# Second attention begun in the first experts' last rounds, and biases of several samples as one block-diagonal product

## The chip, the core and the metric

One core of one Trainium2 chip runs the whole program. The metric is the device time in microseconds, the median of several executions. An execution of the profiler is one more run; its trace is what this document reads. TensorE (PE in the rows, PEld its weight loads) multiplies matrices, VectorE (DVE), ScalarE (ACT) and GpSimd (POOL) work elementwise, SyncE (SP) issues most DMAs. Each engine has its own instruction queue and runs it strictly in the order in which the program wrote it; they meet at semaphores.

## The reference

The input x is 64 samples of 8192 numbers. All is float32.

```python
h = tokenizer(x)                      # conv, batch norm, ReLU, max pool, twice; self-attention; conv, norm
h = h + attention_and_mlp(layernorm(h))   # local and linear attention of 8 heads, then an MLP 64-256-64
h = h + experts(layernorm(h))             # 16 experts 64-128-64, two chosen per token, then a layer norm
h = h + attention(layernorm(h))           # 8 heads of width 64 over 512-token rows, softmax, Wout, bout
h = h + small_experts(layernorm(h))       # 32 experts 64-16-64, one chosen per token

# the part of experts() that the change touches:
topk_vals, topk_idx = top_k(x @ gate_w + gate_b, 2)
topk_w = softmax(topk_vals)
expert_out = relu(x @ w1 + b1) @ w2 + b2
y = x + sum(topk_w * expert_out[topk_idx])
out = (y - mean(y)) / sqrt(var(y) + eps) * gamma + beta
```

After the tokenizer, the data are 64 samples of 128 tokens with 64 features each. The kernel treats each sample of 128 tokens for itself: a sample is one tile of 128 partitions by 64.

## The kernel before

The kernel is written instruction by instruction, with an own program for each engine. It is a row of stages, in the list `PHASES`: tokenizer, a norm, first attention (`attention0`), a norm, MLP (`mlp0`), a norm, first experts (`experts0`), a norm (`n5`), second attention (`attention1`), a norm, last experts (`experts1`). Every stage gives each engine a function, and an engine's program is those functions one after another. So the order of the work on an engine is the order in which the code was written, and an engine passes from one stage to the next by itself; only the waits on semaphores hold it. A norm between two stages gathers the per-sample statistics of all 64 samples (VectorE: six small operations and a reciprocal; ScalarE: the square root), so the next stage's input waits for the last group of the stage before.

The tokenizer works in 8 groups of 8 samples (`NG`, `GS`), the others in 16 groups of 4 samples (`TG`, `TS`). Each stage has a `rest(g, b, ...)` per engine, called once for each group, with a hardware loop around the middle groups; steps of neighbouring groups are interleaved there by hand.

- *Tokenizer.* SP loads inputs in halves of a group, two groups ahead; a first block of constants, the rest of the tokenizer's (`load_rest`), and then the constants of all other stages and the experts' weights (`load_layers`). `conv1`, `conv2` and `conv3` are the convolutions on TensorE, `reduce1` and `reduce2` the max pools on VectorE. `fold_w2` prepares the second convolution's weights on VectorE, and stands there ahead of all `reduce1` (L404).
- *First experts.* For each group the input is centred and scaled on GpSimd (`Paired.pool`), transposed on TensorE (`Paired.pe`), copied out by ScalarE (`Paired.act`). `hidden` (L1431) and `out` (L1443) are the products of two experts for four samples; `relu` (L1644) stands between them on ScalarE; `weighted` (L1585) multiplies by the gate weights on VectorE; `add` (L1368, L1371) sums on GpSimd; `fold` (L1397) ends it. `turn_weights` (L1451) transposes the gate weights of each of the four samples, `turned` (L1653) copies them, `biases` (L1459) multiplies each sample's with the experts' output biases `eb2`, in halves of 64 tokens. `sums`, `count_y`, `variance`, `normal`, `result` and `count` on VectorE, `centre` and `scale` on GpSimd and `deviation` on ScalarE are the layer norm, one to two groups later. A `tail` does what is left after the last group.
- *Second attention.* TensorE first multiplies the weights, `wkT` with `wqT` and `wvT` with `wout` (L1893), into two matrices `w_a` and `w_m`, copied out by ScalarE (L1959). GpSimd makes a group's input, `turned` (L1699, L1704, L1812), for two groups ahead of the loop. TensorE transposes it (L1714) and makes four projections (`piece`, L1850 and L1852), each in the same two banks of PSUM, so each waits until ScalarE has copied the one before (L1936, L1941). Then for each sample: scores (`now`, L1862), maximum and difference on VectorE (L1908, L1911), exp on ScalarE (L1948), transposes (`lag1`, L1870), copy (L1953), products with the values (`lag2`, L1884), division (L1916, L1919), and the sums over heads on GpSimd.
- *Last experts.* `biases` (L2049) adds the chosen expert's output bias to each sample from the transposed one-hot matrix, eight products of 64 columns a group.

Each float32 matmul has two records in the trace, each transpose one. `m.ps` is the PSUM, eight banks of 512 columns.

## Time and profile before

| | us |
|---|---|
| median of 3 runs | 1034.19 (1032.43 to 1036.08) |
| the profiled execution | 1035.63 |
| its span, first to last instruction | 1033.8 |
| mean granted TensorE clock in it | 0.949 |
| busy: TensorE, weight loads | 947.3, 689.6 |
| busy: VectorE, ScalarE, GpSimd | 694.2, 639.9, 519.2 |

The profile is one execution. A timeline merges instructions of one line that follow each other: start, duration, engine, line, operation, what is written from what is read, shapes (partitions x elements), how many, and in brackets how long the engine had been idle and what ended that. The stages lie at about 0 to 161 us (tokenizer), to 276 (first attention), to 327 (MLP), to 627 (first experts), to 921 (second attention) and to the end (last experts), as the norms between them show.

### The profile page before, as it was taken

What the parts mean: (1) busy time and instruction counts of PE and PEld (TensorE: products, weight loads), DVE (VectorE), ACT (ScalarE), POOL (GpSimd) and SP (SyncE); (2) the same over time, 40 slices, a digit from 0 to 9 for tenths busy, and PEclk for the clock granted to TensorE, in tenths of its full rate; (3) what the DMA queues carried; (4) which work ended last, traced back from release to release, by engine and by line L of the source; (5) the groups of instructions that cost most, each with busy time, mean ns of one, the idle gap of its engine ahead of it and who ended that gap; (6) DMA issues with size and microseconds to landing.
All of it is one profiled execution on the core that took longest, in us unless ns stands there. A gap on an engine that the chain in (4) does not pass through costs nothing. (4 is left out here: it accounts for less than half of the span.)

```text
span 1033.8 us, 36620 instructions
## 1 busy us (share of the span) xinstructions
PE 947.3 (92%) x13042; PEld 689.6 (67%) x13042; DVE 694.2 (67%) x1930; ACT 639.9 (62%) x1192; POOL 519.2 (50%) x813
## 2 busy tenths in 40 slices
PE   7899976999697999999999986999999999949998
PEld 2354554677475888888888874566666666637887
DVE  5577743777566467777777772788888888854443
ACT  1254553788554677777777752677777777733443
POOL 0001113888473578787878773355555656451210
PEclk8899995999988999999999995999999999978999
DMA  9623000000000000000000000000000000000001
GB/s 268 106 37 56 0 2 1 1 0 0 1 1 1 3 3 3 0 0 0 0 0 0 1 3 0 1 3 1 0 0 0 0 0 0 2 1 17 20 20 27
DMA packets 10770, 14.99 MB, mean 14 GB/s; under 512 B 9296, under 2 KB 9296, under 8 KB 9680
## 3 DMA queue, kind: packets, MB, share of 16 engines
q1 hardware_dynamic: 10608, 13.71, 6.1%
q8 instruction: 42, 0.69, 0.3%
q10 hardware_dynamic: 96, 0.39, 0.2%
q14 instruction: 24, 0.20, 0.1%
HBM read 12.00 MB, written 2.10 MB: 14 GB/s over the span
## 5 line engine op out<-in xcount | busy, mean ns | idle before, releaser
L1644 ACT ACTIVATE e_hid<-ps,cst 128x512 f32<-128x512 f32 x256 | 154.8, 686 | 54.2 <-PE ps L1431 54.0
L1371 POOL TENSOR_TENSOR e_acc<-e_acc,e_part 128x512 f32<-128x512 f32 x96 | 122.0, 1271 | 42.5 <-DVE e_part L1585 35.4
L1443 PEld LDWEIGHTS ps<-ew,e_hid 128*64 128x64 f32 x4096 | 124.6, 138 | 20.9 <-issue 10.9
L1443 PE MATMUL ps<-ew,e_hid 128*64 128x64 f32 x4096 | 133.3, 224 | 0.0
L1431 PE MATMUL ps<-e_xs,ew 64*128 64x256 f32 x1024 | 129.5, 393 | 0.0
L1585 DVE TENSOR_TENSOR e_part<-ps,e_wt 128x512 f32<-128x512 f32 x128 | 86.9, 688 | 57.3 <-PE ps L1443 57.2
L1431 PEld LDWEIGHTS ps<-e_xs,ew 64*128 64x128 f32 x1024 | 94.7, 189 | 15.3 <-issue 3.3
L1908 DVE TENSOR_REDUCE a_rmax<-ps 128x8 f32<-128x1024 f32 x64 | 78.3, 1223 | 36.3 <-PE ps L1862 35.2
L1817 POOL TENSOR_TENSOR a_sum<-a_part 128x256 f32<-128x256 f32 x64 | 46.4, 725 | 106.4 <-DVE a_part L1919 106.4
L1870 PEld LDWEIGHTS ps<-cst,a_ex 128*128 128x128 f32 x512 | 54.9, 140 | 49.7 <-issue 40.6
L1911 DVE TENSOR_TENSOR a_diff<-ps,a_rmax 128x1024 f32<-128x1024 f32 x64 | 78.4, 1225 | 6.6
L218 POOL TENSOR_TENSOR t_prob<-t_ex,t_rscale 128x512 f32<-128x512 f32 x8 | 11.9, 1492 | 135.6 <-DVE t_rscale L437 135.6
L1953 ACT ACTIVATE a_prob<-ps 128x1024 f32<-128x1024 f32 x64 | 65.5, 1024 | 18.2 <-PE ps L1870 18.2
L1862 PE MATMUL ps<-a_u,a_xs 64*128 64x512 f32 x256 | 71.5, 635 | 5.2 <-DVE a_diff L1911 4.4
L2149 ACT ACTIVATE e_hid<-ps,cst 128x512 f32<-128x512 f32 x64 | 38.9, 687 | 58.5 <-PE ps L2031 58.5
L1884 PE MATMUL ps<-a_v,a_prob 128*64 128x66 f32 x2048 | 73.9, 224 | 1.1 <-DVE a_part L1919 1.1
L1884 PEld LDWEIGHTS ps<-a_v,a_prob 128*64 128x64 f32 x2048 | 65.0, 136 | 11.8 <-issue 11.8
L1870 PE MATMUL ps<-cst,a_ex 128*128 128x128 f32 x512 | 70.0, 279 | 1.7 <-ACT a_ex L1948 1.6
L1948 ACT ACTIVATE a_ex<-a_diff 128x1024 f32<-128x1024 f32 x64 | 67.3, 1052 | 3.8 <-DVE a_diff L1911 2.5
L1936 ACT ACTIVATE a_u<-ps 128x1024 f32<-128x1024 f32 x32 | 32.8, 1025 | 34.3 <-PE ps L1850 34.3
L694 POOL TENSOR_TENSOR e_xn<-e_xc,norm_rstd 128x256 f32<-128x256 f32 x32 | 21.8, 682 | 63.6 <-PE ps L706 62.6
L414 DVE TENSOR_REDUCE c_max<-ps 128x128 f32<-128x1024 f32 x32 | 39.0, 1223 | 14.8 <-PE ps L241 14.5
(259 smaller groups left out, 2043.3 us busy)
## 6 DMA issues: line engine op xcount, KB each, us to landing
x_in<-x_dram SPq DMA_DIRECT2D x45, 128.0 KB, 5.0
cst<-cst_dram SPq DMA_DIRECT2D x1, 3005.0 KB, 18.1
out_dram<-e_res SPq DMA_DIRECT2D x16, 128.0 KB, 1.9
ew<-ew_dram SPq DMA_DIRECT2D x1, 1024.0 KB, 19.6
cst<-cst_dram SPq DMA_DIRECT2D x1, 704.0 KB, 9.9
ew<-ew_dram SPq DMA_DIRECT2D x1, 512.0 KB, 20.5
x_in<-x_dram ACTq DMA_DIRECT2D x3, 128.0 KB, 6.0
cst<-cst_dram SPq DMA_DIRECT2D x1, 329.5 KB, 5.3
```

The lines of the kernel that those rows point to most:

```text
L1371: eng.tensor_tensor(acc[:, :, :, :], acc[:, :, :, :], part[n % RING][:, :, :, :], ALU.add).then_inc(sum_sb.sem, 1)
L1431: mm = eng.matmul(m.ps[:, 2 + 2 * (n % 2) + r, j * 256:(j + 1) * 256], w1[rows, e * F0:(e + 1) * F0], T.xs[b][rows, :], start=True, stop=True)
L1443: mm = eng.matmul(m.ps[rows, 6 + n % 2, to:to + C], hid[e % 8][:, a:a + C], w2[:, e * C:e * C + C], start=True, stop=True)
L1585: eng.tensor_tensor(part[n % RING][:, :, :, :], m.ps[:, 6 + n % 2, :].rearrange("p (s j c) -> p s j c", s=TS, j=2), wt[b][:, :, 2 * n:2 * ...
L1644: nc.scalar.activation(hid[e % 8][:, :].rearrange("p (r t) -> p r t", r=2), m.ps[:, 2 + 2 * (n % 2):4 + 2 * (n % 2), j * 256:(j + 1) * 256 ...
L1862: mm = eng.matmul(m.ps[:, 2 + h, :], T.xs[b][rows, s * P:(s + 1) * P], u[b][rows, s, :, :].rearrange("p h t -> p (h t)"), start=True, stop ...
L1870: mm = eng.transpose(m.ps[:, 4 + j // 4, (j % 4) * P:(j % 4 + 1) * P], ex[s % 2][:, j, :], col(m, "ident"))
L1884: mm = eng.matmul(m.ps[rows, 6 + j // 4, (j % 4) * P:(j % 4) * P + W], prob[s % 2][:, j, rows], v[b][:, s, head * V:head * V + W], start=T ...
L1908: eng.tensor_reduce(rmax[:, :], src, AX, ALU.max).then_inc(max_sb.sem, 1)
L1911: eng.tensor_tensor(diff[:, :, :], src, bc(rmax[:, :], [P, H, P]), ALU.subtract).then_inc(diff_sb.sem, 1)
L1948: nc.scalar.activation(ex[s % 2][:, :, :], diff[:, :, :], ACT.Exp).then_inc(exp_sb.sem, 1)
L1953: nc.scalar.activation(prob[s % 2][:, :, :], m.ps[:, 4:6, :].rearrange("p a (j t) -> p (a j) t", t=P), ACT.Identity).then_inc(prob_sb.sem, 1)
```

## The change

- *First experts.* The gate weights of four samples are transposed at once: a tile of 128 tokens by 4 x 16 weights becomes 64 rows by 128. The bias matrix `eb2` is block-diagonal, 64 rows by 4 x 64 columns, so one product per half of 64 tokens gives the biases of all four samples.
- *Last experts.* The two bias blocks `fb20` and `fb21` lie next to each other, so one product serves two samples.
- *Second attention.* Its weight products are made by TensorE in the tokenizer's last two rounds (`weights`) and copied at the end of the tokenizer's ScalarE program. The norm `n5` is computed in two parts: for the first 48 samples in the last but one round of the first experts, for the late 16 in the second attention's first round. GpSimd makes the attention's input for group 0 in the last but one experts round and for group 1 in the last; TensorE transposes group 0's and makes its first projection in the last experts round. For group 0 the four projections have banks of their own (`START`). What the experts' tail had for the last group (`normal`, `result`, `count`, `scale`, `deviation`) is passed on in `m.left` and placed in the attention's first round.
- *Fillers.* `busy` issues products of 128 x 128 by 512 columns whose result nobody reads: 5 ahead of the first attention, 3 ahead of the MLP, 5 ahead of the first experts, 8 ahead of the last.
- *Tokenizer.* SP waits for the first constants before it issues the rest; the second convolution of group 0 goes ahead of group 1's first; `fold_w2` goes behind group 0's `reduce1`.
- *Memory.* Semaphores are reused one stage later than before, and unused tiles put the first attention and both expert stages at other addresses than their neighbours, so that a stage may begin while the one before it ends.

The diff, cut to what the prediction speaks of:

```diff
-         ("eb2", C), ("gamr", C), ("betr", C)]
+         ("eb2", TS * C), ("gamr", C), ("betr", C)]
...
     def sp(eng):
         load_half(eng, 0, 0, 0)
+        eng.wait_ge(m.cst_sem, 16)
         m.load_rest(eng)
...
+        def weights(part):
+            d = slice(0, C)
+            if part == 0:
+                eng.wait_ge(m.cst2_sem, 16)
+                eng.wait_ge(conv1_max.sem, conv1_max.at(NG - 1))
+            for h in range(2 * part, 2 * part + 2):
+                out, dup = slice(h * C, (h + 1) * C), slice(h * P, (h + 1) * P)
+                for bank, l, r in ((0, "wkT", "wqT"), (1, "wvT", "wout")):
+                    mm = eng.matmul(m.ps[:, bank, out], col(m, l, d)[:, dup], col(m, r, d)[:, out],
+                                    start=True, stop=True)
+            if part == 3:
+                mm.then_inc(m.a1_weights_ps, 1)
...
             eng.wait_ge(m.cstb_sem, 16)
+            conv2(0, 0)
             conv1(1, 1, 0)
-            conv2(0, 0)
             conv1(1, 1, 1)
...
             if among(g, 1, NG - 2):
                 conv1(g + 1, 1 - b, 3)
+            if not among(g, 0, NG - 1):
+                weights(2 * (g - NG))
             if among(g, 2, NG + 1):
                 conv3(g - 2)
+            if not among(g, 0, NG - 1):
+                weights(2 * (g - NG) + 1)
...
             for h in range(4):
                 reduce1(0, 0, h)
+            fold_w2()
+            reduce2(0, 0)
             reduce1(1, 1, 0)
-            reduce2(0, 0)
+            reduce2(0, 1)
             reduce1(1, 1, 1)
-            reduce2(0, 1)
...
-        fold_w2()
         steps(eng, first, rest)
...
         steps(eng, first, rest)
+        eng.wait_ge(m.a1_weights_ps, 1)
+        for n, scale in ((0, float(C / HEADS) ** -0.5), (1, 1.0)):
+            nc.scalar.activation(m.a1_weights[n][:, :], m.ps[:, n, :], ACT.Identity,
+                                 scale=scale).then_inc(m.a1_weights_sb, 1)
...
+        stat = m.stat_last
+        samples = (slice(0, S - late), slice(S - late, S)) if late else (slice(0, S),)
...
+        def variance(eng, n=0):
+            sl = samples[n]
+            eng.wait_ge(stat[0], stat[n - len(samples)])
...
+def busy(eng, m, bank, n):
+    for _ in range(n):
+        eng.matmul(m.ps[:, bank, :], col(m, "ident"), m.cst[:, 0:512], start=True, stop=True)
...
                    start=True, stop=True).then_inc(pre, 1)
+        busy(eng, m, 4, 5)
...
+        eng.wait_ge(m.a1_weights_sb, 2)
...
+        busy(eng, m, 2, 3)
         eng.wait_ge(pre_sb, 2)
...
+    wT = sb("wT", [P, P])
     hid = [sb(f"hid{n}", [P, NT]) for n in range(8)]
...
+    m.h_last, m.h_rounds = h_sb, TG - 1
+    m.stat_last = (h_stat.sem, h_stat.at(TG - 5), h_stat.at(TG - 1))
+    m.base_last, m.banks_last = (base_sb.sem, base_sb.at(TG - 1)), (part_sb.sem, part_sb.at(TG - 1))
...
                 eng.wait_ge(base_sb.sem, base_sb.at(g))
                 T.scale(eng, g + 2, b)
+            else:
+                m.early["pool"](eng, 1 - more, 1 - more)
             add(g, 5)
...
         def tail(g, b):
             scale(g - 1)
             centre(g)
-            scale(g)
+        m.left["pool"] = lambda: scale(TG - 1)
...
-            for s in range(TS):
-                mm = eng.transpose(m.ps[0:E, 1, s * P:(s + 1) * P], wt[b][:, s, :], col(m, "ident"))
-            mm.then_inc(wT_ps.sem, 1)
+            settle(eng, m)
+            eng.transpose(m.ps[0:TS * E, 1, 0:P], wt[b][:, :, :].rearrange("p s e -> p (s e)"),
+                          col(m, "ident")).then_inc(wT_ps.sem, 1)
...
-            for s in range(TS):
-                for rows in HALVES:
-                    a = s * P + rows.start
-                    mm = eng.matmul(m.ps[rows, 1, s * C:(s + 1) * C], wT[:, a:a + C], col(m, "eb2"),
-                                    start=True, stop=True)
+            for rows in HALVES:
+                mm = eng.matmul(m.ps[rows, 1, 0:TS * C], wT[:, rows], col(m, "eb2"), start=True, stop=True)
...
+                if k == 2 and not more:
+                    m.early["turned"](eng)
+                if k == 6 and not more:
+                    m.early["piece"](eng)
                 out(g, b, k + 1)
...
+        busy(eng, m, 2, 5)
         eng.wait_ge(m.ew1_sem, 16)
...
+                if n == 0 and more == 1:
+                    m.parts["n5"][0](eng, 0)
+                if n == 4 and more == 1:
+                    m.parts["n5"][2](eng, 0)
...
+        m.left["dve"] = {0: lambda: normal(TG - 1), 1: last, 2: lambda: m.parts["n5"][0](eng, 1)}
...
+            nc.scalar.activation(wT[0:TS * E, :], m.ps[0:TS * E, 1, 0:P], ACT.Identity).then_inc(wT_sb.sem, 1)
...
+                if e == 9 and more == 1:
+                    m.parts["n5"][1](eng, 0)
+                if e == 9 and not more:
+                    m.early["copied"](eng)
...
+        m.left["act"] = lambda: deviation(TG - 1)
...
+    START = (2, 4, 0, 6)
...
-    w_a, w_m = sb("w_a", [P, H * C]), sb("w_m", [P, H * C])
+    w_a, w_m = m.a1_weights
...
+                if first and s in after:
+                    after[s]()
+        for k in range(done, 4 if piece else 0):
             piece(0, 0, k)
+        if "prologue" in after:
+            after["prologue"]()
         rest(0, 0, first=True)
+        if "round" in after:
+            after["round"]()
         rest(1, 1)
...
+    def turned_pool(eng, g, b):
+        if g == 0:
+            eng.wait_ge(*T.norm)
+        turned_norm(eng, g, b)
+    def turned_norm(eng, g, b):
+        T.pool(eng, g, b)
+        sl = bass.ds(g * TS, TS)
+        eng.wait_ge(T.norm_sb.sem, T.norm_sb.at(g, 1))
+        settle(eng, m)
+        eng.tensor_tensor(m.h[:, sl, :], m.h[:, sl, :],
+                          col(m, "boutr").unsqueeze(1).broadcast_to([P, TS, C]), ALU.add).then_inc(base_sb.sem, 1)
...
-        eng.wait_ge(*T.norm)
-        rounds(eng, ("lag2", "x1"), turned, early=1, lag2=lag2)
+        m.left["pool"]()
+        rounds(eng, ("lag2", "x1"), turned, early=1, after={"round": lambda: eng.wait_ge(T.norm[0], 4)}, lag2=lag2)
...
+    def piece_pe(eng, g, b, k):
+        first = isinstance(g, int) and g == 0
+        bank = START[k] if first else 0
+        if k == 0 or first:
+            eng.wait_ge(T.xs_sb.sem, T.xs_sb.at(g))
+        else:
+            eng.wait_ge(uv_sb.sem, uv_sb.at(g, k))
+        if first and k == 0:
+            eng.wait_ge(m.a1_weights_sb, 2)
+        if first and k == 2:
+            eng.wait_ge(*base_last)
+        if first and k == 3:
+            eng.wait_ge(*banks_last)
+        for r, rows in enumerate(HALVES):
+            n = 2 * (k % 2) + r
+            sl = slice(n * P, (n + 1) * P)
+            if k < 2:
+                mm = eng.matmul(m.ps[:, bank + r, :], w_a[rows, sl], T.xs[b][rows, :], start=True, stop=True)
+            else:
+                mm = eng.matmul(m.ps[:, bank + r, :], T.xs[b][rows, sl], w_m[rows, :], start=True, stop=True)
+        mm.then_inc(uv_ps.sem, 1)
+    m.early["turned"] = lambda eng: T.pe(eng, 0, 0)
+    m.early["copied"] = lambda eng: T.act(eng, 0, 0, score_ps)
+    m.early["piece"] = lambda eng: piece_pe(eng, 0, 0, 0)
...
-            eng.wait_ge(uv_sb.sem, uv_sb.at(g, 3 + s // 2))
+            eng.wait_ge(uv_sb.sem, uv_sb.at(g, 4 if isinstance(g, int) and g == 0 else 3 + s // 2))
...
-        eng.wait_ge(*m.banks_last)
-        d = slice(0, C)
-        for h in range(H):
-            out, dup = slice(h * C, (h + 1) * C), slice(h * P, (h + 1) * P)
-            for bank, l, r in ((2, "wkT", "wqT"), (3, "wvT", "wout")):
-                mm = eng.matmul(m.ps[:, bank, out], col(m, l, d)[:, dup], col(m, r, d)[:, out], start=True, stop=True)
-        mm.then_inc(w_ps, 1)
-        def prepare():
-            eng.wait_ge(w_sb, 2)
-            eng.wait_ge(ones_set, 4)
-        rounds(eng, ("now", "x0", "lag1", "x1", "lag2", "x2"), turned, piece, prepare=prepare,
+        eng.wait_ge(ones_set, 4)
+        rounds(eng, ("now", "x0", "lag1", "x1", "lag2", "x2"), turned, piece, done=1,
...
+        after = dict(m.left["dve"])
+        after["round"] = lambda: m.parts["n5"][2](eng, 1)
+        rounds(eng, ("now", "lag3", "lag2"), lambda g, b: None, after=after, now=now, lag2=lag2, lag3=lag3)
...
+            bank = START[k] if isinstance(g, int) and g == 0 else 0
...
-        eng.preload_act_table(ACT.Exp)
-        eng.wait_ge(w_ps, 1)
-        for w, src, scale in weights:
-            nc.scalar.activation(w[:, :], src, ACT.Identity, scale=scale).then_inc(w_sb, 1)
-        rounds(eng, ("x0", "lag1", "x1", "now", "x2"), turned, piece, now=now, lag1=lag1)
+        after = {"prologue": m.left["act"], "round": lambda: m.parts["n5"][1](eng, 1)}
+        rounds(eng, ("x0", "lag1", "x1", "now", "x2"), turned, piece, after=after, now=now, lag1=lag1)
...
-            for s in range(TS):
+            a = AT["fb20"][0]
+            for p in range(TS // 2):
                 for rows in HALVES:
-                    a = s // 2 * P + rows.start
-                    eng.matmul(m.ps[rows, 5, s * C:(s + 1) * C], hotT[b][:, a:a + C], col(m, f"fb2{s % 2}"),
-                               start=(s == 0), stop=False)
+                    t = p * P + rows.start
+                    eng.matmul(m.ps[rows, 5, 2 * p * C:2 * (p + 1) * C], hotT[b][:, t:t + C], m.cst[:, a:a + 2 * C],
+                               start=(p == 0), stop=False)
...
+        busy(eng, m, 3, 8)
         lagged(eng, TG, ahead, rest)
...
+PHASES = [(tokenizer, 0), (norm("n1", twice=True), 0), (attention0, 56576), (norm("n2"), 0), (mlp0, 0),
+          (norm("n3"), 0), (experts0, 67712), (norm("n5", 4 * TS), 0), (attention1, 0), (norm("n6"), 0),
+          (experts1, 67712)]
...
+                    m.mem.enter_context(nc.sbuf_tensor(f"neighbour{n}", [P, below // 4], F32))
                 m.steps = []
                 phases.append(make(nc, ctx, m))
-            m.ended += m.steps
+            if m.steps:
+                m.ended += older
+                older = m.steps
...
+    put("eb1", f0("b1").T)
+    own = np.zeros((TS, EXPERTS0, TS, C), np.float32)
+    for s in range(TS):
+        own[s, :, s, :] = f0("b2")
+    put("eb2", own.reshape(TS * EXPERTS0, TS * C))
```

## Rows read from the trace of the kernel before

**Rows 1.** The page's share of the span by engine, busy us and instructions.

```profile
PE 947.3 (92%) x13042; PEld 689.6 (67%) x13042; DVE 694.2 (67%) x1930; ACT 639.9 (62%) x1192; POOL 519.2 (50%) x813
```

**Rows 2.** Timeline, TensorE, a first-experts round: start, us, engine, line, out<-in, count [idle].

```profile
500.90 0.64 PE L1459 MATMUL ps<-cst,e_wT 128*64 128x64 f32 x16
514.13 0.60 PE L1451 MATMUL ps<-cst,e_wt 128*16 128x128 f32 x4
518.50 0.64 PE L1459 MATMUL ps<-cst,e_wT 128*64 128x64 f32 x16
```

**Rows 3.** Timeline, TensorE, four 128-column products into 64 rows, two lots in a row.

```profile
185.51 0.39 PE L935 MATMUL ps<-a_lprobT,a_v 128*64 128x128 f32 x4
185.73 0.39 PE L933 MATMUL ps<-a_qsT,a_ctxm 128*64 128x128 f32 x4
```

**Rows 4.** Chain that ended last, last stage: start, us, what, count.

```profile
933.82 3.41 PE ps L2031 x16
948.11 1.73 PE ps L2031 x16
950.21 0.62 PE ps L2049 x16
```

**Rows 5.** Timeline, TensorE, from the first experts' end into the second attention.

```profile
612.70 4.03 PE L1443 MATMUL ps<-ew,e_hid 128*64 128x64 f32 x128
621.94 7.09 PE L1893 MATMUL ps<-cst 64*128 64x64 f32 x32 [5.21 <-DVE y L1498]
644.73 1.92 PE L1862 MATMUL ps<-a_u,a_xs 64*128 64x512 f32 x4
649.24 1.13 PE L1862 MATMUL ps<-a_u,a_xs 64*128 64x512 f32 x4 [1.54 <-DVE a_diff L1911]
```

**Rows 6.** Timeline, VectorE and GpSimd, the same stretch.

```profile
614.71 5.50 POOL L1371 TENSOR_TENSOR e_acc<-e_acc,e_part 128x512 f32<-128x512 f32 x4
621.04 0.84 DVE L1498 TENSOR_TENSOR y<-e_fold,e_base 128x256 f32<-128x256 f32 x1 [1.95 <-POOL e_fold L1397]
623.83 0.61 DVE L587 BATCH_NORM_STATS2 stat<-h 128x6 f32<-128x64 f32 x4
646.70 1.23 DVE L1908 TENSOR_REDUCE a_rmax<-ps 128x8 f32<-128x1024 f32 x1 [17.43 <-PE ps L1862]
```

**Rows 7.** Timeline, GpSimd: first and last step of a second-attention input group.

```profile
629.47 0.61 POOL L1699 TENSOR_TENSOR a_xc<-h,norm_mean 128x256 f32<-128x256 f32 x1 [2.05 <-DVE norm_rstd L618]
631.26 0.63 POOL L1812 TENSOR_TENSOR h<-h,cst 128x256 f32<-128x256 f32 x1
```

**Rows 8.** Stretches: us, busy of PE PEld DVE ACT POOL, granted clock, DMA, GB/s.

```profile
619.00:622.00 3.00, 0.06 (x1) 0.06 (x1) 1.01 (x3) 0.00 (x0) 2.53 (x3) 0.78 0.00 0
646.00:649.00 3.00, 1.69 (x6) 0.71 (x4) 2.27 (x2) 0.61 (x2) 0.00 (x0) 0.66 0.02 5
647.00:913.00 266.00, 259.07 (x3046) 166.36 (x3045) 217.65 (x313) 196.57 (x202) 140.47 (x285) 1.00 0.00 1
```

**Rows 9.** Timeline, TensorE, the MLP's first hidden product and its third.

```profile
282.27 2.08 PE L1203 MATMUL ps<-m_xs,wm1s 64*128 64x256 f32 x8 [0.52 <-ACT m_xs L713]
289.83 1.13 PE L1203 MATMUL ps<-m_xs,wm1s 64*128 64x256 f32 x8
```

**Rows 10.** Timeline, ScalarE, a table load and what follows it.

```profile
505.65 1.28 ACT L1633 ACT_TABLE_LOAD   x1
506.94 0.20 ACT L1633 ACTIVATE e_gexp<-e_gap 128x4 f32<-128x4 f32 x1
```

**Rows 11.** Timeline, the tokenizer's last convolution, and the first experts' memset on GpSimd.

```profile
156.35 3.73 PE L274 MATMUL ps<-x,cst 64*128 64x256 f32 x16 [0.86 <-DVE x L447]
329.77 0.53 POOL L1405 MEMSET e_wT<- 128x512 f32 x1 [11.45 <-DVE norm_rstd L618]
```

**Rows 12.** Timeline, TensorE, group 2's first convolution; and a stretch as in rows 8.

```profile
32.60 1.13 PE L241 MATMUL ps<-x_in,w1s 48*128 48x512 f32 x4 [0.33 <-DVE c_max L414]
30.00:32.00 2.00, 2.00 (x13) 1.24 (x12) 0.77 (x1) 0.69 (x1) 0.00 (x0) 0.95 0.33 57
```

More of the change, by code:

```diff
@@ L627, in act @@
         def act(eng):
[L628 to L629 removed]
+            deviation(eng)
             if twice:
```

116 lines of the change are left out of this document (47 added, 69 removed).

## Prediction

> **What bounds the kernel now.** I read the page's shares first: TensorE is busy 947.3 of 1033.8 us [rows 1]. Matmul busy time is modelled, so this says only where to look. The kernel is a chain of stages, and I then read three timelines of it: a steady round of the stages that hold most of the time, the seam between each pair of stages, and the chain that ended last for the final stage.
>
> In a steady round of the first experts TensorE runs from one product to the next without a listed wait, and the round repeats from 500.90 to 518.50, in 17.6 us [rows 2]. There are 16 such rounds. The last stage is the same: its chain is TensorE work alone, round after round [rows 4]. So in both a matmul taken out shortens the round, as long as no other engine is near it; ScalarE, VectorE and GpSimd are at 62, 67 and 50% of the span [rows 1].
>
> At the seams it is different. From the end of the first experts' products (612.70 + 4.03 = 616.73) to the second score product that follows a finished softmax difference (649.24), TensorE does only the weight products, one group's transposes, four projections and one score, with gaps between, and it does them at the lower of its two clocks [rows 5, 8]. VectorE waits 17.4 us for the first scores, at 646.70 [rows 6]. This seam is the largest thing in the profile that isn't work.
>
> **The change, part by part.** All sums are against the profiled run: 1035.63 us, of which 1033.8 are its span; it lies 1.44 above the median of 1034.19, so I take the difference off the median.
>
> *Gate weights and biases of the first experts.* One transpose for four: four take 0.53 us (0.60 less the tail that overlaps the next product), so one takes 0.13: 0.40 saved. Sixteen 64-column passes, 0.57 us net of the tail [rows 2], become four of 256 columns. For their pace I have 128 columns into 64 rows, four in 185.73 - 185.51 = 0.22 us, 55 ns each [rows 3], hence 110 ns for 256, 0.44 for four: 0.13 saved. Together 0.53 a round, 16 rounds: **-8.5**. Bounds: -4 if another engine takes over half of it, -10 if the ScalarE copy (16 rows by 512 becomes 64 by 128) helps too.
>
> *Biases of the last stage.* Sixteen passes in 0.62 [rows 4] become eight of 128 columns, 0.44 at 55 ns: 0.18 over 16 rounds, -2.9; as the neighbours may set the pace I take **-2.5** (bounds 0 and -3).
>
> *The seam into the second attention.* The two weight products move to the tokenizer. The transposes and the first projection of group 0 move into the last experts round, and the other projections get banks of their own, so they needn't wait for ScalarE's copies. TensorE: the transposes at full clock (0.53, like the four above) and a projection (two products of 512 columns, as the score's, 1.13 less its tail: about 1.0 [rows 5]) lie ahead of the last expert's output product, so it ends at 618.2; three projections in sequence end at about 621. GpSimd: its last adds run without a pause from 614.71 to 620.21 [rows 6], so this queue is full. A group's input steps last 629.47 to 631.89, 2.4 us [rows 7]; group 1's now stand between these adds. Some of it overlaps with the later last product, so the fold is some 2.0 later and VectorE's tail, 621.04 to 624.44 [rows 6], ends at 626.4. Only then does VectorE come to the first maximum, since the scores (about 621.8) are there: 646.70 - 626.4 = 20.3 gained.
>
> Given back: (a) TensorE stands idle from 621.8 until the first difference ends, 626.4 + 2.5 = 628.9 (from the first maximum to the score that waits for the difference, 646.70 to 649.24 [rows 5, 6]). After 616.73 the granted clock averaged 0.78 in 619 to 622, so it had fallen at about 620.7, 4 us after the last product; this gap is 7, so it falls here too. A score then takes 1.92 instead of 1.13 [rows 5], and the next projection and transposes double likewise: 2.5 (bounds 0 and 6). (b) Left-over steps of the last experts (normalise, result, count, the late 16 samples' variance) now sit between maxima and differences in VectorE's queue. Behind them wait the next maximum, then TensorE, which needs the score banks. They are the 3.4 us tail's kind of work, partly in VectorE's waits for scores: 1.5 (bounds 0 and 3.5). (c) ScalarE now takes three table loads after the start (exp, square root, exp) at 1.28 each [rows 10]; about 1.5 of them shows, since the differences wait for exp's buffer (bounds 0 and 4). Net **-14.8**, bounds -20 and -7.
>
> The row shows no more than 1.28: the exp starts 0.01 us after its load [rows 10]. The Trainium skill (ScalarE: Activation LUTs, What ACT_TABLE_LOAD costs) counts a drain of about 1.38 us with every switch. By it, three switches would cost 4.1 more, and the seam would give -10.7. This trace disagrees for a switch between Relu and exp.
>
> *Weight products in the tokenizer's tail.* 32 passes took 7.09 at the low clock [rows 5]; in four pieces they are 0.9 each at full clock or 1.8 at the low. Three have waits of VectorE or ScalarE to hide in; the third delays the last convolution by up to 0.9 if the clock is low. Two copies on ScalarE stand ahead of the norm's square root. Against it, more work there may keep the clock up for that convolution, 3.73 at the low clock [rows 11], 1.9 less at full. I take **0**, bounds -2.5 and +2.5.
>
> *Filling products* at four stage starts. They run where TensorE waits for a norm, and the stage begins at full clock if they reach up to it. A hidden product of the MLP is 2.08 at the start and 1.13 two groups on [rows 9]; the last stage's first is 3.41 against 1.73 [rows 4]. If the clock holds, the MLP's three groups give about 3. But the starts of first attention and last stage are sparse, and the clock may fall again before their long products. I take: attention -1, MLP -2, experts -1.1 (of it 0.4 from the smaller memset, 0.53 before [rows 11], and 0.4 from the single transpose), last stage -1.1: **-5.2**, bounds +2 (filler at low clock runs past its gap) and -11.
>
> *The start.* The tokenizer's constants wait for the first ones, so inputs of group 0 land sooner, and VectorE no longer stands at the fold ahead of its maxima. But group 2's first convolution came at 32.60, and the DMA queue had only just run empty then (share 0.33 in 30 to 32) [rows 12]: bytes cap the gain at some 1.5. SP's queue behind the new wait holds all further loads, but those in flight cover it. **-1**, bounds +1 and -3.
>
> Everything else has one answer: the renumbered semaphores and the unused tiles that move others apart issue nothing, and the 192 more columns of constants lie ahead of group 2's inputs in the queue, within the bound just given.
>
> **Sum:** -8.5 - 2.5 - 14.8 + 0 - 5.2 - 1.0 = -32.0. Span 1001.8, profiled run 1003.6, median **1002**.
>
> **Rivals.** *Fast starts.* The fillers keep the clock through all four starts and through the tokenizer's tail: 6 more from the fillers, 2 from the tail: 994. For: 4 us of gap before the clock fell. Against: in 646 to 649 it was still at 0.66 [rows 8], though the first scores had started at 644.73 [rows 5].
>
> *Slow seam.* GpSimd's full queue and the low clock take more: the bounds of (a) to (c) together, -7 instead of -14.8: 1010.
>
> *The overlap doesn't come about.* The early transposes stand in TensorE's queue ahead of expert products and wait for GpSimd; if that is late by a whole input step (2.4) at each of the three places, and VectorE's tail stretches as much, the seam gives nothing like 20 but some 3: 1014.
>
> *Slower.* The low clock of the seam stays. In the second attention at half clock, each group's TensorE work doubles: 266 us at clock 1.00 for 16 groups, 259 of them busy [rows 8], so 16.6 a group. Here nothing dense stands ahead of the first scores any more. Two groups at low clock cost 33, as much as the whole gain; the third makes it slower, about 1045. For: the clock stayed low from 620.7 to 648. Against: in those 27 us TensorE was sparse, and after three dense products it rose.
>
> *The page's drain* would give 1006 by the sum above; it is inside my range.
>
> **How the numbers follow.** Forecast (996 to 1007) 0.57; fast starts 0.15; slow seam 0.16; drain 0.04; overlap fails 0.05; slower 0.03. The range takes the forecast, the fast starts down to 991 and the slow seam to 1012. About 0.3% is what a measurement of this kernel can tell from no change. Faster 0.95, same 0.02 (between the failed overlap and the low clock of two groups), slower 0.03.
>
> **What would show it.** In the profile after: a first-experts round of 17.07 us; a last-stage round of 0.62 reduced to 0.44 in its biases; VectorE's first score maximum some 8 us after the last expert's output product instead of 30; the third table load in the second group of attention; the MLP's first hidden product at 1.1 us; group 2's convolution near 31. The prediction is wrong if the round stays near 17.6, if the clock row after the seam stays at half for more than two groups, or if TensorE waits for GpSimd inside the last experts round.

## The result, and the profile after

The changed kernel takes 1019.25 us in the median of four runs (1015.97 to 1020.00), the kernel before 1034.16: ratio 0.984, 95% interval 0.982 to 0.987. The forecast was 1002. The sign was right, and more than half of the forecast gain (17 of 32 us) is missing. The profiled execution took 1020.0 us, its span is 1018.1.

The page's shares barely move: TensorE's busy time is even 2.9 us longer than in [rows 1], though 326 of its instructions are gone.

```profile
PE 950.2 (93%) x12716; PEld 680.0 (67%) x12716; DVE 700.6 (69%) x1937; ACT 636.3 (62%) x1195; POOL 519.7 (51%) x813
```

Where the time went is seen by the starts of the same instructions in every profile: VectorE's first operation of each norm, the bias products of the first and the last experts. These are the stretches between them, in us, for the kernel before, the changed one and the twelve experiments below. The sixth stretch runs from the last bias product of the first experts to the norm behind the second attention, so the sixteenth round and the seam are in it. The seventh is a part of it, from the same start to VectorE's first maximum.

| kernel | tokenizer | first attention | MLP | start of first experts | 15 rounds of them | seam and second attention | to the first maximum | start of last experts | 15 rounds of them |
|---|---|---|---|---|---|---|---|---|---|
| before | 162.10 | 115.04 | 50.45 | 14.85 | 263.83 | 315.08 | 40.43 | 16.43 | 90.48 |
| changed | 164.35 | 114.63 | 47.35 | 13.61 | 258.45 | 307.70 | 28.12 | 16.24 | 90.15 |
| changed_again | 163.61 | 113.09 | 47.35 | 15.25 | 258.45 | 306.06 | 27.71 | 15.23 | 89.98 |
| merges_alone | 162.47 | 113.50 | 50.71 | 14.33 | 258.42 | 315.02 | 40.37 | 16.40 | 89.98 |
| no_fillers | 162.14 | 112.78 | 51.22 | 14.53 | 258.45 | 305.04 | 26.65 | 16.50 | 90.00 |
| two_fillers | 164.92 | 112.81 | 48.28 | 15.24 | 258.52 | 306.04 | 27.75 | 15.44 | 89.99 |
| start_order | 161.03 | 112.46 | 48.30 | 15.22 | 258.44 | 307.41 | 27.89 | 16.23 | 90.09 |
| no_sp_wait | 165.15 | 114.50 | 47.35 | 13.61 | 258.45 | 304.96 | 26.52 | 16.23 | 89.97 |
| ones_late | 162.00 | 114.64 | 47.35 | 13.62 | 258.44 | 300.93 | 21.37 | 16.23 | 90.11 |
| seam_filler | 166.84 | 114.47 | 47.36 | 13.61 | 258.47 | 298.10 | 21.37 | 16.25 | 89.98 |
| late_inverse | 163.11 | 114.58 | 47.36 | 13.60 | 258.46 | 298.61 | 21.32 | 16.10 | 89.98 |
| combined | 162.01 | 115.81 | 47.36 | 15.19 | 258.52 | 297.42 | 21.37 | 16.23 | 90.10 |
| combined_new_order | 163.35 | 115.81 | 49.80 | 13.62 | 258.52 | 297.45 | 21.42 | 16.12 | 89.98 |
| combined_last_filled | 160.99 | 112.78 | 48.27 | 15.25 | 258.44 | 297.44 | 21.41 | 14.60 | 89.98 |

From before to changed: +2.3 tokenizer, -0.4, -3.1, -1.2, -5.4, -7.4, -0.2, -0.3, and +0.1 behind the last bias product: -15.7, the difference of the spans. The table also shows what one profile can't price. Unchanged code differs by up to 3 us in the first attention and 5 in the tokenizer, as the clock happens to fall; the rounds of both expert stages repeat within 0.2. The sixth stretch differs too where its code is the same: in the six profiles from changed to no_sp_wait that have this seam (all but merges_alone), it is 305.0 us where the low clock behind the last bias product lasts 10.2 us in all (no_fillers, no_sp_wait), 306.0 to 306.1 at 13.7 (changed_again, two_fillers) and 307.4 to 307.7 at 17.1 (start_order, changed). So the changed kernel's -7.4 is at the poor end of -7.4 to -10.1.

*A round of the first experts.* The changed kernel's timeline of TensorE (columns as in [rows 2]): from one bias product to the next it is 17.24 us.

```profile
495.16 0.60 PE L1511 MATMUL ps<-cst,e_wT 128*64 128x256 f32 x4
495.69 0.63 PE L1474 MATMUL ps<-cst,e_xs 128*128 128x32 f32 x4
...
508.36 0.27 PE L1505 MATMUL ps<-cst,e_wt 128*64 128x128 f32 x1
508.56 2.00 PE L1485 MATMUL ps<-e_xs,ew 64*128 64x256 f32 x16
...
512.40 0.60 PE L1511 MATMUL ps<-cst,e_wT 128*64 128x256 f32 x4
```

Start to start, the one transpose takes 0.20 (508.36 to 508.56) where four took 0.53, and the four passes of 256 columns 0.53 (495.16 to 495.69), where sixteen of 64 took 0.56.

*The seam.* TensorE, GpSimd, VectorE and ScalarE in the changed kernel:

```profile
609.76 1.15 PE L1497 MATMUL ps<-ew,e_hid 128*64 128x64 f32 x32
...
611.53 4.08 POOL L1423 TENSOR_TENSOR e_acc<-e_acc,e_part 128x512 f32<-128x512 f32 x3
615.69 0.72 POOL L1451 TENSOR_TENSOR e_fold<-e_acc 128x256 f32<-128x256 f32 x1
618.88 0.69 POOL L1397 TENSOR_TENSOR e_yc<-y,e_y_mean 128x256 f32<-128x256 f32 x1 [1.87 <-DVE e_y_var L1572]
619.66 0.10 POOL L1903 MEMSET a_v<- 128x4 f32 x1
619.83 2.08 PE L1925 MATMUL ps<-a_xs,a_w_a 64*128 64x512 f32 x4 [8.92 <-POOL a_v L1903]
625.11 1.35 PE L1949 MATMUL ps<-a_u,a_xs 64*128 64x512 f32 x4
626.51 1.23 DVE L1983 TENSOR_REDUCE a_rmax<-ps 128x8 f32<-128x1024 f32 x1 [6.65 <-PE ps L1949]
...
644.94 1.28 ACT L647 ACT_TABLE_LOAD   x1
646.57 0.25 DVE L652 RECIPROCAL norm_rstd<-norm_dev 128x16 f32<-128x16 f32 x1 [2.69 <-ACT norm_dev L647]
649.22 1.70 PE L1949 MATMUL ps<-a_u,a_xs 64*128 64x512 f32 x4 [2.48 <-DVE a_diff L1986]
```

The last expert product ends at 610.9, and the second projection starts at 619.83, 8.92 us later, released by a memset. That is the wait for `ones_set`, four small memsets that write the ones into the value buffers. The wait stood ahead of the projections in the kernel before too; there the weight products and the norm covered it (the memsets are over at 627.4, the first transposes start at 631.4). GpSimd reaches the memsets only behind the last adds, the fold and the centring. None of the projections reads those buffers. Meanwhile the clock falls (stretches as in [rows 8]):

```profile
612.00:614.00 2.00, 0.00 (x0) 0.00 (x0) 0.99 (x4) 0.00 (x0) 1.85 (x2) 1.00 0.01 4
616.00:618.00 2.00, 0.00 (x0) 0.00 (x0) 1.48 (x6) 0.00 (x0) 1.01 (x2) 0.50 0.00 0
622.00:624.00 2.00, 2.00 (x6) 0.72 (x6) 0.00 (x0) 1.32 (x2) 0.00 (x0) 0.50 0.00 0
```

*The MLP's start* runs at full clock now: its first hidden product takes 1.13 us, 2.08 in [rows 9].

```profile
283.86 1.13 PE L1253 MATMUL ps<-m_xs,wm1s 64*128 64x256 f32 x8 [0.52 <-ACT m_xs L761]
```

### The profile page after: what moved, and what is told of

It reads as the page before. It is cut to its first block and busy times, and to the rows that moved or that the text cites. A ratio compares the mean times of both kernels' runs of the same rounds, so it can differ in the third digit from the quotient of the medians.

```text
span 1018.1 us, 35564 instructions
## 1 busy us (share of the span) xinstructions
PE 950.2 (93%) x12716; PEld 680.0 (67%) x12716; DVE 700.6 (69%) x1937; ACT 636.3 (62%) x1195; POOL 519.7 (51%) x813
## 6 DMA issues: line engine op xcount, KB each, us to landing
ew<-ew_dram SPq DMA_DIRECT2D x1, 1024.0 KB, 15.2
```

## The experiments

All times are medians of device time, with the range in brackets. Beside the experiments the kernel before took 1035.8 us, and the changed kernel, run again beside the last three, 1020.38.

### The wait for the ones

```diff
-        eng.wait_ge(ones_set, 4)
         rounds(eng, ("now", "x0", "lag1", "x1", "lag2", "x2"), turned, piece, done=1,
...
         def lag2(g, b, s):
+            if isinstance(g, int) and g == 0 and s == 0:
+                eng.wait_ge(ones_set, 4)
```

> The changed kernel, with TensorE's wait for the ones of the value buffers (ones_set, four memsets on GpSimd) moved from ahead of group 0's last three projections to ahead of the first product that reads those buffers. Theory: this wait is what holds the start of the second attention. In the profile after, TensorE is idle from 610.8 to 619.83, released by the memset that ends at 619.76, and GpSimd comes to it only behind all adds of the last experts and its centring. Without it the projections end at about 614, the first score at about 615, and VectorE takes its first maximum when its tail ends, at 619.85 instead of 626.51: 6.7 us less, 1012.6 against 1019.3. Rival: VectorE's left-over steps and the table loads of ScalarE bound the first rounds; then less than 2 us come, 1017 to 1019. Second rival: the idle time just moves behind the first score, the clock falls there, and half of it is lost: 1016.

Measured: 1011.49 (1010.79 to 1013.40), ratio to before 0.975 (0.971 to 0.979), 7.8 less than the changed kernel. The theory stands: against the profile of the changed kernel the stretch to the first maximum is 6.75 us shorter, as expected (6.7); against the other five profiles of that seam it is 5.2 to 6.5. In ones_late's timeline the projections follow the last expert product at once. VectorE comes to the first maximum when its tail ends, at 617.42:

```profile
608.46 1.13 PE L1925 MATMUL ps<-a_xs,a_w_a 64*128 64x512 f32 x4
609.42 1.88 PE L1927 MATMUL ps<-a_w_m,a_xs 64*128 64x512 f32 x8
611.14 1.03 PE L1949 MATMUL ps<-a_u,a_xs 64*128 64x512 f32 x4
...
617.42 1.21 DVE L1984 TENSOR_REDUCE a_rmax<-ps 128x8 f32<-128x1024 f32 x1
619.93 2.08 PE L1949 MATMUL ps<-a_u,a_xs 64*128 64x512 f32 x4 [6.72 <-DVE a_diff L1987]
```

### The merges alone

The kernel before with the hunks of the diff for `turn_weights`, `biases` (both stages), `turned` and `eb2`.

> The kernel before with the merges alone: one transpose for the gate weights of four samples, the block-diagonal bias product in the first experts, and one bias product for two samples in the last. Theory now: a merged product costs what its columns cost, and the weight loads that fall away were hidden. By the profiles of before and after a round of the first experts goes from 17.605 to 17.245 and one of the last from 6.10 to 6.076, so 16 rounds of each give 5.8 + 0.4 = 6.2 us, 1028.0 against 1034.2. As predicted blind it would be 11.0, 1023.2. Rival: alone, without the rest of the change, the round may fall to 17.07 since GpSimd's and ScalarE's queues are as before; then 8.5 + 0.4, 1025.3.

Measured: 1029.05 (1027.72 to 1031.72), ratio 0.992 (0.990 to 0.995), 6.7 less than before. Fifteen rounds of the first experts fell from 263.83 to 258.42, those of the last from 90.48 to 89.98, as in the changed kernel; the price of the prediction is out, and so is the rival that other queues held the round back.

### The order of the start, and SyncE's wait

```diff
+            conv1(1, 1, 0)
             conv2(0, 0)
-            conv1(1, 1, 0)
...
+            reduce1(1, 1, 0)
             reduce2(0, 0)
-            reduce1(1, 1, 0)
+            reduce1(1, 1, 1)
             reduce2(0, 1)
-            reduce1(1, 1, 1)
```

> The changed kernel with the order of the start as before: the first quarter of group 1's first convolution ahead of group 0's second convolution on TensorE, and its maximum ahead of the second pooling on VectorE; the fold of the weights and SyncE's wait stay as changed. Theory: in the profile after, group 2's first convolution comes 2.4 us later than before, because the quarters of group 1's convolution are a chain through VectorE's maxima of 2.54 us each, and one quarter more now stands behind the second convolution. Then 2.4 us come back, 1016.9 against 1019.3, and group 2's first convolution is at 32.5 or earlier. Rival: the delay comes from SyncE's wait, which holds group 1's inputs, or from the clock, which was at half for 18 to 22 and 25 to 32 in the profile after; then less than 1 us comes: 1018.5 to 1019.3.

Measured: 1017.06 (1016.64 to 1017.96), 2.2 less than the changed kernel; the tokenizer ended at 161.03, and group 2's first convolution came at 31.79. The clock as the rival isn't out by this run: it was at full here all through 22 to 42 us. More on it stands under *Together*.

```diff
-        eng.wait_ge(m.cst_sem, 16)
         m.load_rest(eng)
```

> The changed kernel without SyncE's wait for the first constants. Up to the tokenizer's end the six profiles so far differ by 3 us: its norm begins at 162.1 in the kernel before, 164.4 in the changed one, 162.0 and 162.1 in two runs with the same code for the start, 162.5 with the start of before and other changes behind it, 161.0 with the old order. Theory: the wait is worth nothing that can be seen at the end of the tokenizer: total within 1.5 of 1019.3, norm between 161.5 and 164.5. Rival: it is what holds the start back, and 1.5 to 2.5 us come back (1017). Third: it was worth the predicted 1 us, and the time rises to 1020.3 or more.

Measured: 1018.60 (1017.69 to 1021.53), tokenizer 165.15. The wait is worth nothing that can be seen, as expected. A single profile can't price the start (same code: 162.0 to 166.8), so the order was tried once more, in the pair of the last group.

### The fillers

no_fillers takes out the four `busy` calls, two_fillers those ahead of the first attention and the last experts.

> The changed kernel without its filling products at the four stage starts. Theory: only the filler ahead of the MLP (the clock stays at full through the start) and the one ahead of the first experts pay; by the profiles of before and after the MLP with its start gave 3.1 us and the first experts' start 1.2. So the whole kernel loses 3.5 to 4.5, 1023.3 against 1019.3, with the MLP's first hidden product back at 2.1 us, and the starts of first attention and last experts unchanged within 0.5. Rival: the fillers hold the clock up for the first attention and the last experts too and what they give there is hidden by something else: then these starts get 1 to 2 us longer each, and the total is 1026. Third: the fillers cost as much as they give: within 1 us.

> The changed kernel without the fillers ahead of the first attention and of the last experts; those ahead of the MLP and the first experts stay. Theory: ahead of the first attention the filler keeps the clock at full only while TensorE waits; it then falls at 171 and is low until 182 in the stage's first products, where without it the low stretch began at 162 and ended at 173. So dropping it gives 1.8 us there, dropping the last one costs 0.3: 1017.8 against 1019.3. Rival: these two are neutral and the difference between the profiles is one of chance: 1018.8 to 1019.8.

Measured: 1020.85 (1018.07 to 1022.54) and 1018.73 (1017.00 to 1022.97), against 1019.25 and 1020.38 for the changed kernel. So by the medians, whose ranges overlap, all four are worth about 1 us of 1019, and two of them nothing. By the table the MLP with its filler takes 47.35 us in seven profiles, 48.3 in three and 49.8 in one, and 50.45 to 51.22 in the three without: mostly 3 to 4 us, and never nothing. The start of the first experts takes 13.6 us with its filler in six profiles and 15.2 in five, where the clock is low once more for 3.4 us, between 332 and 340; without it, 14.3 to 14.9. So the 1.2 that the first two profiles gave it is a matter of where the clock falls. In the first attention the filler seemed to cost 1.8 (114.6 against 112.8): it puts off the fall of the clock, which then mostly comes within the stage's first sparse products. But changed_again, with the filler, took 113.09, and combined, without it, 115.81. That expectation was drawn from too few profiles. What holds is the place of the low stretch, the changed kernel's and no_fillers' stretches:

```profile
170.00:180.00 10.00, 7.35 (x28) 4.62 (x28) 3.07 (x7) 4.19 (x17) 5.67 (x11) 0.59 0.01 2
...
282.00:290.00 8.00, 6.22 (x65) 3.88 (x64) 2.68 (x8) 3.63 (x8) 7.44 (x12) 1.00 0.00 1
912.00:922.00 10.00, 6.41 (x38) 4.76 (x36) 4.92 (x32) 1.83 (x4) 2.37 (x4) 0.52 0.01 2
```

```profile
162.00:173.00 11.00, 3.92 (x15) 2.39 (x14) 5.08 (x19) 3.80 (x7) 4.62 (x9) 0.54 0.00 0
280.00:289.00 9.00, 8.48 (x58) 5.82 (x60) 1.95 (x8) 3.14 (x6) 7.45 (x12) 0.50 0.01 3
```

With a filler the clock is at full through the MLP's start in the seven profiles with 47.35 us; in the three with 48.3 it is low for 3.4 us, and in combined_new_order, with 49.8, for 6.8 (279.3 to 286.1). In the starts of the first attention and the last experts it falls all the same, some 7 us later: 7.4 and 6.4 us behind the start of the norm in the changed kernel (171.8, 912.5), 0.7 behind and 0.7 ahead of it in no_fillers (162.8, 903.5).

### What the seam gives back

seam_filler is ones_late with six fillers in TensorE's gap behind the first score.

```diff
         rounds(eng, ("now", "x0", "lag1", "x1", "lag2", "x2"), turned, piece, done=1,
+               after={0: lambda: busy(eng, m, 4, 6)},
```

> The kernel with the late wait for the ones, and six filling products on TensorE behind group 0's first score, where it stands idle for 6.7 us before the second one (613.2 to 619.93) and the clock falls at 616.2, to come back at 623.8. Theory: the low clock of the first samples costs what its dense products take more: of the second score, a projection and transposes, some 2.3 us between 619.93 and 624.6 on the chain; kept at full clock, the second attention starts 2 us sooner: 1009.5 against 1011.5. Rival: as in the first attention, the filler only puts off the fall; the clock then falls within the sparse second and third sample, and nothing or up to 1 us is lost: 1011.5 to 1012.5.

Measured: 1009.20 (1007.97 to 1012.54), 2.3 less than ones_late, with ranges that overlap; the stretch to the norm fell by 2.8, from 300.93 to 298.10. The clock never left full in this seam; ones_late's stretch at the second score, and then seam_filler's, whose seam lies 4.7 us later:

```profile
620.00:622.00 2.00, 2.00 (x6) 0.97 (x8) 0.43 (x1) 0.97 (x1) 1.26 (x3) 0.50 0.00 0
```

```profile
624.00:626.00 2.00, 1.36 (x6) 0.69 (x8) 1.28 (x4) 1.06 (x1) 0.74 (x2) 1.00 0.00 0
```

late_inverse is ones_late with VectorE's reciprocal and GpSimd's wait for it one round later:

```diff
-        after["round"] = lambda: m.parts["n5"][2](eng, 1)
+        after["round1"] = lambda: m.parts["n5"][2](eng, 1)
```

> The kernel with the late wait for the ones, and VectorE's reciprocal for the 16 late samples' norm (with GpSimd's wait for it) moved from between group 0 and group 1 to behind group 1. The square root on ScalarE with its two table loads stays where it is. Theory: VectorE's 2.69 us wait for that square root holds the next maximum and difference, then TensorE's score, 2.47 us idle at 640.11, and the low clock of 640.3 to 643.5 behind it (1.5 to 2 us more). With it gone 2 to 4 us come back: 1008.5 against 1011.5. Rival: ScalarE's 2.9 us for square root and table loads hold the exp instead, which TensorE's transposes need, and the gain is under 1 us: 1011.

Measured: 1010.85 (1009.18 to 1013.17), 0.6 less than ones_late, with ranges that overlap. In the profile the stretch is 2.3 shorter (298.61), and TensorE's 2.47 us of waiting turned into 1.33, now for the exponential behind the table load:

```profile
642.44 1.07 PE L1959 MATMUL ps<-cst,a_ex 128*128 128x128 f32 x8 [1.33 <-ACT a_ex L2029]
```

So both the theory (2.3 in the profile) and the rival (0.6 in the median) have something for them. The two edits don't add: combined has both and reaches 297.42, 3.5 below ones_late, where the single ones gave 2.8 and 2.3. Both take away the same second low stretch of ones_late (640.4 to 643.9). In ones_late, and then in seam_filler, the score behind that wait:

```profile
640.11 1.79 PE L1949 MATMUL ps<-a_u,a_xs 64*128 64x512 f32 x4 [2.47 <-DVE a_diff L1987]
```

```profile
643.61 1.13 PE L1949 MATMUL ps<-a_u,a_xs 64*128 64x512 f32 x4 [2.47 <-DVE a_diff L1988]
```

The wait is the same, 2.47 us, and the clock stays at full in seam_filler. From this score to the product with the values ones_late takes 4.6 us (to 644.70) and seam_filler 2.9 (to 646.55): some 1.6 us, which is what the sum of the two gains has too much.

### Together

combined is ones_late with seam_filler's and late_inverse's edits and start_order's order, without the first attention's filler.

> The changed kernel once more, beside the next three: its own median on this chip and the spread of its start. Expected 1019.3, within 1 us. In the profile, the part from the tokenizer's norm to the first experts' last bias product should repeat within 1 us (the stretches of low clock aside), and the tokenizer's end anywhere between 162 and 167.

> The changed kernel with: late wait for the ones, six fillers behind group 0's first score, the late samples' reciprocal behind group 1, the first attention's filler taken out, and the old order of the start. If the single gains add up: 1019.3 - 7.8 (ones) - 2.3 (seam fillers) - 0.6 to 2.3 (reciprocal) - 1.0 (first attention) - 2.2 (order) = 1003.7 to 1005.4. If the order's gain was one of chance: 1006.5. If reciprocal and seam fillers remove the same low clock only once: up to 1 us more.

> The same as combined, but with the order of the start as in the changed kernel. Theory: the order costs 2 us, since one quarter more of group 1's first convolution is left behind group 0's second one, and each waits for the maximum of the one before: 2 us above combined. Rival: the ten profiles' start scatters by 5 us with the arrival of the first inputs, and the order is worth nothing: within 0.7 us of combined.

Measured: changed_again 1020.38 (1016.49 to 1020.77), combined 1008.27 (1006.57 to 1010.58), combined_new_order 1011.72 (1008.18 to 1012.54). The gains don't add up to 1005: the second low stretch was counted twice, and the first attention had its slow start in both profiles (115.81), which are among the slower of their five runs.

The order gives 3.5 in the median here, with ranges that overlap, and gave 2.2 above. In the profiles, the tokenizer ended at 160.99 to 162.01 in three profiles with the old order, and at 162.00 to 166.84 in nine with the new one (with no_sp_wait). Input isn't what scatters: the first convolution starts at 9.1 to 10.1 in all twelve. The low clock is: in the nine, the end of the tokenizer goes up with the time at low clock between 8 and 60 us, from 13.7 us of it (162.00, 162.14) to 24 (166.84). At 13.7 us the old order ended at 161.03 and 160.99, and at 162.01 in combined, where the clock was low for 3.6 us more in the last 10. So about 1 us is the order itself, and the rest goes with the clock. In all nine the clock falls once between 23 and 34 us, and in none of the three; whether the waits of the new order bring that about, no run parts. The changed kernel, and combined:

```profile
26.00:31.00 5.00, 3.76 (x6) 1.34 (x7) 2.41 (x2) 0.23 (x1) 0.00 (x0) 0.50 0.93 182
```

```profile
22.00:42.00 20.00, 15.53 (x92) 6.14 (x84) 12.93 (x11) 5.85 (x19) 0.00 (x0) 1.00 0.69 168
```

In combined_new_order the quarters of group 1 follow the second convolution one by one, each waiting for VectorE's maximum:

```profile
20.38 1.13 PE L242 MATMUL ps<-x_in,w1s 48*128 48x512 f32 x4
22.91 1.74 PE L242 MATMUL ps<-x_in,w1s 48*128 48x512 f32 x4 [1.41 <-DVE c_max L433]
25.97 2.08 PE L242 MATMUL ps<-x_in,w1s 48*128 48x512 f32 x4 [1.32 <-DVE c_max L433]
```

In combined the first of them ran at 16.83, ahead of the second convolution.

> The same as combined, with four more fillers in the start of the last experts, three behind the second group's transpose and one behind the first one-hot transpose, where TensorE stands idle for 2.65 and 0.94 us and the clock falls at 912.7, to come back at 922.6. Theory: the first hidden product then takes 1.8 instead of 3.6 us and the small ones before it half: 2.5 to 3.5 us less than combined. Rival: the fillers stand in TensorE's queue ahead of what the chain through VectorE needs and delay it by about what the clock gives: within 1 us of combined.

```diff
+            if isinstance(g, int) and g == 0:
+                busy(eng, m, 3, 3)
             if back:
                 biases(g - 1, 1 - b)
             if left is not None:
                 turn_hot(g, b)
+            if isinstance(g, int) and g == 0:
+                busy(eng, m, 3, 1)
```

Measured: 1006.49 (1004.88 to 1008.18), ratio to before 0.971 (0.969 to 0.974), the best of all, 1.8 less than combined, with ranges that overlap: less than the 2.5 to 3.5 of the theory, more than the rival's 1. The start of the last experts fell from 16.23 to 14.60, a stretch that is 15.2 to 16.5 in all other profiles; the first hidden product takes 1.93 us at 905.54, and 3.65 in combined. Here the added fillers stood in the gaps of the sparse chain itself, not only ahead of it.

## Why the prediction was right in sign and wrong in size

Three steps failed: the price of the merged passes, a wait that holds the seam and was not looked at, and the sign of the start. Of what was to show it, the third table load in the second group (644.94) and the MLP's first product came as named. A round of the first experts is 17.24 instead of 17.07, the last stage's bias group 0.59 instead of 0.44, and VectorE's first maximum comes 15.6 us behind the last expert product (610.9 to 626.51), not 8. That 626.51 is nearly the 626.4 of the forecast is luck: the rounds ahead of it had ended sooner. Group 2's first convolution came at 34.98, not near 31 (32.60 before). None of the three signs of being wrong came: the round isn't near 17.6, the low clock behind the seam is over in less than two groups (at 653.1), and TensorE waits for GpSimd behind the last experts round, not in it.

*Merges of the first experts* (forecast -8.5, measured -5.7): the step that failed is the price of the passes. I read 0.57 us for sixteen passes as their own time, and then priced four wide ones at 0.44 by their columns alone. Both groups have 1024 columns, 0.44 us at the 55 ns per 128 of [rows 3], and both measured about 0.1 more (0.56 and 0.53). As the rest is the same for one group as for the other, the merge saves 0.03, not 0.13. Likewise the four transposes' 0.53 holds such a rest: three of them save 0.33, 0.11 each, and the last still takes 0.20. The Trainium skill (TensorE: Matmul & The Clock Gate, Wait — 56ns, not 53.3ns?) gives a matmul its columns over 2.4 GHz and 2.5 ns: by it 12 fewer passes save 0.03 us, and the trace agrees (0.56 to 0.53). The remaining 0.1 lies behind the last product of a group: within the group the starts of 256-column products are 0.22 us apart, and from the last to the next kind of product it is 0.32; with 64 columns 0.06 and 0.16. What it is made of isn't shown.

*Merges of the last experts* (-2.5, measured -0.4 to -0.5): the same step; the group goes from 0.61 to 0.59 us.

*The seam* (-14.8, measured -7.4, and -7.7 to -10.1 in the five other profiles of the same seam): the sum of what the seam gives was right within 1.2, and one wait was overlooked. I wrote that the early scores would be there at 621.8 and that VectorE would come to them when its tail ended, 20.3 us earlier. In ones_late it is 19.1 earlier (40.43 to 21.37; the tail itself ends 3.2 later in its round than before, not 2.0), and the whole stretch is 14.1 shorter. The changed kernel reached 12.3 of the 20.3 (the five others 12.5 to 13.9), because TensorE stood at `ones_set`, behind GpSimd's full queue. The diff showed that line, and I had even said that GpSimd's queue is full; the step left out was to ask of every wait ahead of the moved projections who fulfils it, and when. What is given back came out near the forecast: 5.5 in all, measured 4.9 (from the first maximum to the norm 274.65 before, 279.56 in ones_late). Of that the forecast gave the low clock 2.5, and seam_filler measured 2.3 to 2.8. It gave VectorE's and ScalarE's left-over steps 3.0; late_inverse moved 0.6 to 2.3, and of the 2.3 some 1.6 is low clock again, so how much the steps themselves cost stays open.

*The page's drain*, the 1.38 us that the Trainium skill (ScalarE: Activation LUTs, What ACT_TABLE_LOAD costs) counts for each switch of tables, had a chance as a rival. In the changed kernel an exponential begins 0.01 us behind its load again, at the switch from the square root too:

```profile
627.76 1.28 ACT L2026 ACT_TABLE_LOAD   x1
629.05 1.06 ACT L2026 ACTIVATE a_ex<-a_diff 128x1024 f32<-128x1024 f32 x1
```

*Weight products in the tokenizer's tail* (0): no run has them alone. The tokenizer of merges_alone, without them, ends at 162.47, those of start_order and combined, with them and the old order, at 161.03 and 162.01; a cost of more than 1 us isn't seen.

*The start* (-1.0): the wrong sign, +1.3 by the profiles (162.1 and 162.5 with the start of before, a middle value of 163.6 with the new one), and 2.2 to 3.5 of cost for the order by the medians, of which about 1 is the order at a like clock. I asked only what the earlier second convolution wins and what bytes allow. The step left out was the chain between TensorE and VectorE into which the moved quarter falls, and a low clock in it that was given no term.

*The fillers* (-5.2 with the start of the first experts): between before and changed the four starts gave 4.9, near the forecast. Taking all fillers out costs only 0.5 to 1.6 in the median and 3.2 to 4.1 by the four starts, so part of the 4.9 was a matter of where the clock fell in those two executions. Where I gave each start something, only the MLP's gain repeats.

Merges and seam ended within the bounds that I gave each (-4 to -10, -20 to -7), the start outside its own. The range missed since it let one term at a time go to its end: seam (7.4), merges (4.9) and start (3.3) all went the same way. The rival *slow seam* had -7 for the seam, and the changed kernel's profile -7.4. That is luck: the rival had it by low clock and left-over steps, which cost what the forecast itself said, and the other profiles have more; its 1010 isn't reached either, since the other terms failed too. The 1045 of *Slower* doesn't follow from its own numbers: three groups at 16.6 each on top of 1002 are 1052.

## What to carry to other kernels

When work is moved ahead of a stage boundary, list every wait that stands between its old and its new neighbours, also those that it doesn't touch, and write beside each which queue fulfils it and when; a wait that cost nothing behind a long gap becomes the bound. A merged matmul is worth the columns it drops: price it from the difference of two whole groups, start to start, not from passes of another place. A filling product paid here where it reached up to dense work; ahead of a sparse chain it mostly moved the low clock to a later place, and fillers in the chain's own gaps took it away. Two edits that remove the same low stretch don't add.

## What was not expected of the hardware

The first attention took 112.5 to 113.5 us in six profiles and 114.5 to 115.8 in eight, in two steps with nothing between, and either kind has profiles with the filler and without it. In start_order, two_fillers, no_fillers and combined_last_filled, of the first kind, the low stretch was over 10.8 to 10.9 us behind the start of the norm, in changed_again 6.7; in all eight of the second kind 17.6 to 20.4 us behind it. merges_alone (113.50) lies between: low until 17.4 us behind it, with 3.4 us at full within. An execution in which the clock rises at another moment differs by 2 to 3 us, more than most single edits here, so medians of several runs, or stretches that repeat, have to carry such terms.
